# Scatters of the last ten expert groups without TensorE signals: a decoder layer with routed experts on one core

## What is computed

```python
logits = xf @ gate_w.T
top_p, top_i = jax.lax.top_k(softmax(logits), 2)
w = top_p / sum(top_p)
for e in range(8):
    g = silu(xf @ gate_proj_w[e].T)      # 128 -> 256
    u = xf @ up_proj_w[e].T
    out += comb[:, e] * ((g * u) @ down_proj_w[e].T)
```

## Time and profile before

| | us |
|---|---|
| timed executions, median of 3 | 948.38 (944.0 to 951.24) |
| profiled execution, its own time | 953.16 |
| span from first to last instruction in it | 951.3 |
| mean granted clock of TensorE | 0.935 |
| TensorE matmuls busy | 835.6 |
| GpSimd busy | 540.2 |

### The profile page before, as it was taken

One profiled execution on the slowest core, in us unless ns is written; L12 is line 12 of the kernel. 1 busy time (PEld: TensorE's weight loads), 2 busy tenths in 40 slices (PEclk: granted clock), 3 DMA queues, 4 the chain that ended last, 5 costly groups with the idle time before them and its releaser, 6 DMA issues.

```text
span 951.3 us, 25572 instructions
## 1 busy us (share of the span) xinstructions
PE 835.6 (88%) x9107; PEld 634.4 (67%) x9107; DVE 643.2 (68%) x2064; ACT 464.5 (49%) x772; POOL 540.2 (57%) x747
## 2 busy tenths in 40 slices
PE   4799999999999999999999999962699998899893
PEld 3577777777667777777777777752466665666662
DVE  5888999889657877777788777654255453445542
ACT  1456657667366766666676665541232221222220
POOL 3466666656532266666666665556266566366665
PEclk8999999999999999999999999975699999889996
DMA  7259960000000011111000000111444354446440
GB/s 239 89 177 390 390 222 0 0 1 1 1 2 14 14 58 59 59 45 36 28 28 31 29 30 28 48 32 40 163 125 120 107 153 126 124 141 212 132 158 5
DMA packets 50336, 87.01 MB, mean 91 GB/s; under 512 B 12809, under 2 KB 28105, under 8 KB 50232
## 3 DMA queue, kind: packets, MB, share of 16 engines
q1 hardware_dynamic: 37872, 72.18, 22.9%
q0 software_dynamic: 11264, 12.70, 4.1%
q10 hardware_dynamic: 1096, 0.73, 0.2%
HBM read 42.08 MB, written 58.41 MB: 106 GB/s over the span
## 4 chain that ended last, share of the span: by engine, by line
PE 58%; issue 7%; DVE 6%; ACT 3%; another core or an unknown queue 3%; POOL 1%; POOLq 0%; DVEq 0%; ACTq 0%
PE psum L1924 12%; PE psum L1936 8%; PE psum L1448 8%; PE psum L1428 7%; PE psum L1409 5%; PE psum L1431 2%; PE psum L1459 2%; PE psum L1471 2%; PE psum L1391 2%; DVE h L1876 2%; PE psum L1395 1%; PE psum L1918 1%; PE psum L1465 1%; PE psum L626 1%
## 5 line engine op out<-in xcount | busy, mean ns | idle before, releaser
L1823 POOL DMA_INDIRECT out<-yo,token x160 | 159.2, 995 | 113.5 <-issue 56.6
L852 POOL DMA_INDIRECT dispatched<-z,idx x128 | 129.6, 1012 | 76.4 <-issue 47.1
L1286 ACT ACTIVATE PT<-psum,key_bias 77x1024 f32<-77x1024 f32 x128 | 136.1, 1105 | 68.2 <-PE psum L1431 67.5
L1428 PE MATMUL psum<-qT,Kb 32*77 32x128 f32 x2048 | 143.6, 300 | 3.6 <-issue 3.5
L1905 ACT ACTIVATE act_g<-psum 128x512 f32<-128x512 f32 x80 | 45.7, 596 | 182.1 <-PE psum L1924 56.0
L978 DVE TENSOR_REDUCE top_score<-psum 128x8 f32<-128x616 f32 x128 | 101.9, 796 | 33.2 <-PE psum L1409 32.7
L1409 PE MATMUL psum<-Kb,qT 32*128 32x308 f32 x512 | 110.3, 503 | 1.5 <-issue 0.5
L1428 PEld LDWEIGHTS psum<-qT,Kb 32*77 32x77 f32 x2048 | 104.8, 156 | 7.2 <-issue 6.4
L1936 PE MATMUL psum<-down,h 128*128 128x128 f32 x640 | 86.6, 293 | 20.7 <-issue 11.0
L1861 DVE SCALAR_TENSOR_TENSOR yo<-psum,xin,base 128x128 f32<-128x128 f32 x156 | 44.0, 344 | 88.8 <-PE psum L1936 46.5
L1431 PE MATMUL psum<-MT,minus_sel 32*77 32x128 bf16 x1024 | 99.6, 228 | 0.5 <-issue 0.5
(11 more groups left out here) (177 smaller groups left out, 1763.8 us busy)
## 6 DMA issues: line engine op xcount, KB each, us to landing
dispatched<-zeros SPq DMA_DIRECT2D x40, 522.0 KB, 7.3
xin<-dispatched SPq DMA_DIRECT2D x40, 522.0 KB
out<-zeros SPq DMA_DIRECT2D x20, 256.0 KB, 3.2
first<-out SPq DMA_DIRECT2D x20, 256.0 KB
X<-in_x SPq DMA_DIRECT2D x16, 256.0 KB, 2.8
out<-X SPq DMA_DIRECT2D x16, 256.0 KB
out<-yo,token POOLq DMA_INDIRECT x160
ctx<-in_ctxT SPq DMA_DIRECT2D x4, 616.0 KB, 6.5
```

What stands on the lines that cost most here:

```text
L852: pool.indirect_dma_start(xg[k], bass.IndirectOffsetOnAxis(ap=idx[n % Z4][:, t, k:k + 1], axis=0), z4[n % Z4][:, t, :], None, bounds_check ...
L1286: nc.scalar.activation(PT[j % 2][:, half * HB * 2 * P:(half + 1) * HB * 2 * P], T[:, 2 * half:2 * half + 2, :].rearrange("p a c -> p (a c) ...
L1428: nc.tensor.matmul(T[:, q, h * P:(h + 1) * P], Kb[par][rows_of(q), h, j * S2:(j + 1) * S2], qT[g % 3][rows_of(q), j * P:(j + 1) * P], star ...
L1823: pool.indirect_dma_start(rows_out if slot else out, bass.IndirectOffsetOnAxis(ap=token[i][:, t:t + 1], axis=0), yo[i][:, t, :], None, bou ...
```

## The change

```diff
                     m = n + 2
-                    paced = m < NE - 1 and n not in (SECOND - 2, SECOND - 1)
+                    paced = n < NE - 2 * PAIR and n not in (SECOND - 2, SECOND - 1)
                     for t in range(G4):
                         if paced and t == 0:
                             pool.wait_ge(s["gate_ps"], HC * m + 1)
                         if paced and t == 1:
                             pool.wait_ge(s["xT_ps"], m + 2)
                         if paced and t == 2:
                             pool.wait_ge(s["y_ps"], m)
                         if paced and t == 3:
                             pool.wait_ge(s["up_ps"], HC * m + 1)
```

## The result

The changed kernel takes 953.77 us (median of 20, 949.54 to 960.55) and the kernel before 949.07 us (median of 20): a ratio of 1.0042 with a 95% interval of 1.0024 to 1.0060. By the ratio that is 4.0 us more; the two medians lie 4.7 us apart. The forecast was 951.4 us, 3.0 more than the kernel before. The change is clear of noise and within 1%.

The account below looks back on a forecast made before the run. TensorE's 5.66 us per group was taken as the bound, with its postings delayed by long scatter runs. Terms 0 + 0 + 4.1 − 2.0 + 0.9 = +3.0 us took 948.4 to 951.4 us, range 943 to 959.

Parts of the forecast that it names:

- Removed waits, group 30: 28 semaphore waits off the path, and group 30's scatters still queued behind group 29's: 0 us each.
- Group 31: Scatter run grows from seven to eleven; one posting comes 1.4 us earlier, three behind it lose as much: 0 us.
- Groups 32 to 37: Steady part: clean groups of 5.66 us alternate with caught ones of 7.94, 6.8 each against 6.12: +4.1 us.
- The end: Last groups: with group 36's scatters gone early, late consumers come about a microsecond earlier each: −2.0 us.
- The clock: One more stretch at 1.2 GHz after TensorE waits, expected in every second execution: +0.9 us.
- Hidden: Rival: postings have slack on TensorE's path, so only ends of waits shift: 0 ± 2, 948.4 us, chance 0.30.
- The gap clears everything: Rival: runs of exactly four with 1.8 us gaps free the postings: −5.8 us, 942.6 us, chance 0.17.
- Run-on: Rival: from group 31 the backlog becomes one unending run, two stalls costing 14 us: 962.4 us, chance 0.13.

Follow-up runs that it names:

- e6_half: Changed kernel with two scatters in place of four in groups 30 to 36, other rows unwritten, on a slower chip: 937.56 us, ratio 0.9947 to the kernel before.
- e12_mid_short: Changed kernel plus a memset of 1020 columns between second and third scatter of groups 30 to 35: 943.81 us, ratio 1.0009 to the kernel before.
- e5: The changed kernel itself, run again on a chip where the kernel before takes 942.64 us: 946.29 us, ratio 1.0045.
- e4: Changed kernel plus a memset of 8 columns ahead of each scatter in groups 30 to 38, on a faster chip: 893.3 us, ratio 0.9996 to the kernel before.
- e1_half: Changed kernel with two scatters in place of four in groups 30 to 36, on a faster chip: 891.1 us, ratio 0.9979 to the kernel before.

## Why the prediction was right

It rested on one reading, that long runs of scatters make TensorE's postings late, and the mechanism held where it was tested: e6_half takes half of the scatters away and the lateness is gone; e12_mid_short keeps them and breaks the run, and most of the postings in the padded groups are punctual. The terms, from the `yo` of group 30 to the last scatter in the two profiles of the result (63.8 us before, 67.9 after, +4.1):

- *Removed waits, group 30*: 0 forecast. Its scatters started at 882.73 behind group 29's, as said.
- *Group 31*: 0 forecast, measured +1.7 (30 to 32: 16.67 against 14.98 us). This is the term that was mis-sized, and by more than the 1.7: before, these two steps also held the 1.7 us that group 32's down matmuls lost at the lower clock, so the lateness alone grew by about 3.4 (an estimate, 1.7 + 1.7). I moved one posting 1.4 us earlier and three later; in fact GpSimd, then in an unbroken run of eleven (873.48 to 886.56), caught the down posting itself. The matmuls ended at 881.84, and `yo` stood idle for 9.15 us until 889.44:

```profile
873.48 0.97 POOL L1823 DMA_INDIRECT out<-yo,token  x1 [2.02 <-issue]
...
879.89 1.95 PE L1936 MATMUL psum<-down,h 128*128 128x128 f32 x16
...
886.56 0.97 POOL L1823 DMA_INDIRECT out<-yo,token  x1 [0.30 <-issue]
889.44 1.13 DVE L1861 SCALAR_TENSOR_TENSOR yo<-psum,xin,base 128x128 f32<-128x128 f32 x4 [9.15 <-remote]
```

- *Groups 32 to 37*: +4.1 forecast (6.8 us each), measured +3.8 (40.53 against 36.70, 6.75 each). The sum of a pair was right, the split was not: 4.5 and 8.9, not 5.7 and 7.9. While the postings were held TensorE had gone on to the matmuls of the next round, so the `yo` behind a late one comes after 4.53 us and not 5.66, and the next run joins the last to one of eight. Eight starts (7 × 1.28 = 8.95), 2.5 until release and 2.0 to the next scatter are 13.4 for two.
- *The end*: −2.0 forecast, measured −1.4 (10.7 against 12.1). Part of it may be the clock: from 930 to 940 us its mean is 0.82 before and 1.00 after.
- *The clock*: +0.9 forecast. There is one stretch at the lower level in each of the two profiles between 868 and 930 us, and in the changed kernel it fell on idle time. So the term has the wrong sign here, −1.5 to −1.7 (3.52 us for group 32's down matmuls before, against 2.05 for the same ones after and 1.79 for group 34's before), and it is already in the +1.7 of group 31.
- Sum: +3.0 forecast, +4.1 in the profiles, +4.0 measured by the ratio. That it came out so near is in part luck: the steady term is right as a sum of two wrong steps, and group 31, put at nothing, was offset by a clock that gave back where I had it cost. Spans differ by only 1.2 us because all that lies ahead of the `yo` of group 30 was 3.0 us quicker in the second profile (878.43 against 881.40), which the change does not touch.

*Hidden* was wrong on the chips of the result and of e5, and right on the faster kind (e4: 0.9996). I had not seen that it could be both. *The gap clears everything* fell: no run of four stood alone in the first profile, though some did in e5_after, with `yo` punctual behind them. *Run-on* did not come as priced (two stalls, 14 us), but its sign did, a gap of over 10 us, once in each profile of the changed kernel (12.14 and 10.15 us), at the very place that I had named for it. The page "SBUF — State Buffer" of the Trainium skill, section "Who interferes with whom", gives a TensorE that nobody disturbs. e4 agrees (22.40 of 22.40 us busy beside an unbroken run of scatters), e5 against e6 does not, though a late posting need not be a matter of the SBUF ports of which the page speaks. What the postings wait for stays open. Against a busy GpSimd alone stands the one profile of e12; which part of a scatter does it, its issue by GpSimd or the transfers that follow, no run here separates.

## What to carry to other kernels

Signals that seem to hold work back for nothing may be spacing it out: before removing them, look at what stands late beside an unbroken run of the same instruction, and compare the start of each consumer with the end of its matmuls. If spacing is what is wanted, a pause of known length on the issuing engine did part of it here, in one run and without a shown gain over the signals; it has to fit into the engine's slack (here 0.5 us per group), or it comes back at the end. And a gain or cost of half a percent should be seen on more than one chip.

## What was not expected of the hardware

The same kernel takes 893 us on some chips and 942 to 949 on others (893.17 and 893.41; 942.64, 941.71 and 949.07, each a median of 17 or more), and the granted clock hardly differs: 0.957 in e1_half, 0.952 in e6_half. The same number of groups shows part of the difference: 19 paced steps of the first choices take 107.6 us on the one kind and 114.5 to 121.2 on the other. The clock does not explain it: from 690 to 780 us, within those steps, it is 1.00 in e4_pad_each and in the kernel before, and TensorE is busy for 90.00 of 90 us in the one and for 86.18 in the other. About 30 of the 56 us lie ahead of the first `yo` (that of group 0 stands at 656.0 in e1_half and at 685.7 in the kernel before), and no run here looks into them. On the first kind no `yo` stands late by over a microsecond behind its matmuls where VectorE was free for it, even in a run of over twenty scatters; on the second kind 9 to 15 of the 40 do in each profile. What makes a chip one or the other is not known. A memset of 0.13 us between two scatters is free, since it lies in the 0.3 us of issue between them; one of 0.98 us moves the next scatter by 0.83.
